# A four-layer graph network on one core: totals by destination and the first layer joined in one stage

## The reference

```python
h = (x @ W).reshape(N, H, C)                      # H = 4 heads, C = 32
alpha = leaky_relu(s_src[row] + s_dst[col], 0.2)
ex = exp(alpha - m[row])
alpha_n = ex / denom[row]                         # softmax over the edges of one source
msg = alpha_n[:, :, None] * h[col]
out = segment_sum(msg, col, num_segments=N)       # sum over the edges of one destination
x = layernorm(x + out.reshape(N, H * C) + bias)
```

## Time and profile before

| | us |
|---|---|
| median of 3 runs (lowest to highest) | 5147.29 (5142.84 to 5148.02) |
| span of the profiled execution, first to last instruction | 5144.9 |
| stage `gat_sums` in it, 2125.0 to 2191.2 | 66.2 |
| stage `first_layer`, 2191.2 to 2475.7 | 284.5 |
| busy over the span: PE, DVE, ACT, POOL | 3166.0, 3394.4, 2871.6, 3664.3 |

### The profile page before, as it was taken

One profiled execution on the slowest core, in us unless ns is written; L12 is line 12 of the kernel. 1 busy time (PEld: TensorE's weight loads), 2 busy tenths in 40 slices (PEclk: granted clock), 3 DMA queues, 4 the chain that ended last, 5 costly groups with the idle time before them and its releaser, 6 DMA issues. The chain is left out here.

```text
span 5144.9 us, 72170 instructions
## 1 busy us (share of the span) xinstructions
PE 3166.0 (62%) x15758; PEld 2414.5 (47%) x15758; DVE 3394.4 (66%) x11785; ACT 2871.6 (56%) x7156; POOL 3664.3 (71%) x3635
## 2 busy tenths in 40 slices
PE   3555555545652666166476746666988887777774
PEld 3554555523431444155465634544555465555552
DVE  6587566658886777467499973333777776666664
ACT  0114666638874888268367762333555566666663
POOL 5777777767774777378677717776777677777777
PEclk9655555569996888689689978888555599989887
DMA  2336888858872777356478858887677632222222
GB/s 72 78 80 197 250 251 255 251 126 249 251 232 76 226 229 225 96 166 203 133 207 222 222 171 235 225 224 202 197 206 205 180 74 73 72 72 71 71 73 60
DMA packets 820080, 862.65 MB, mean 168 GB/s; under 512 B 161384, under 2 KB 595149, under 8 KB 819227
## 3 DMA queue, kind: packets, MB, share of 16 engines
q1 hardware_dynamic: 703656, 673.59, 42.6%
q0 software_dynamic: 112896, 179.36, 15.5%
q10 hardware_dynamic: 3314, 7.36, 0.4%
HBM read 494.63 MB, written 370.82 MB: 168 GB/s over the span
## 5 line engine op out<-in xcount | busy, mean ns | idle before, releaser
L1929 POOL DMA_INDIRECT gs_xs<-t_t,kept_idx_b x392 | 370.0, 944 | 228.4 <-issue 118.9
L1035 POOL DMA_INDIRECT t_alpha<-gsm_raw,gsm_edge_idx x392 | 386.2, 985 | 165.6 <-issue 117.0
L2193 POOL DMA_INDIRECT mss_xs<-t_x,kept_idx_a x392 | 387.8, 989 | 144.2 <-issue 118.5
L2049 POOL DMA_INDIRECT gs_xs<-t_z,kept_idx_a x392 | 384.5, 981 | 138.3 <-issue 119.2
L2185 POOL DMA_INDIRECT out_dram<-mss_o,kept_scat_idx x392 | 394.9, 1007 | 119.4 <-issue 117.9
L1227 PE MATMUL gsm_hp<-kept_w,gsm_zT 128*128 128x128 f32 x1568 | 252.5, 309 | 357.9 <-ACT gsm_zT L1093 357.5
L1025 POOL DMA_INDIRECT gsm_raw<-t_al,kept_idx_b x392 | 379.0, 967 | 124.5 <-issue 118.5
L1598 POOL DMA_INDIRECT att_xs<-t_t,kept_idx_a x392 | 371.5, 948 | 134.2 <-issue 117.3
L536 POOL DMA_INDIRECT sort_xs<-in_x_dram,kept_src_idx x392 | 379.8, 969 | 119.5 <-issue 119.5
L534 POOL DMA_INDIRECT sort_xd<-in_x_dram,kept_dst_idx x392 | 378.7, 966 | 119.4 <-issue 119.4
L216 PE MATMUL gs_tp<-kept_ident,gs_xs 128*128 128x128 f32 x784 | 277.5, 370 | 263.6 <-DMA gs_xs<-t_t,kept_idx_b 154.6
(11 more groups left out here) (556 smaller groups left out, 11014.5 us busy)
## 6 DMA issues: line engine op xcount, KB each, us to landing
t_t<-sort_o SPq DMA_DIRECT2D x61, 858.0 KB
t_x<-gsm_o SPq DMA_DIRECT2D x196, 264.0 KB
sort_x<-in_x_dram SPq DMA_DIRECT2D x61, 832.0 KB
gsm_x<-t_t SPq DMA_DIRECT2D x196, 256.0 KB
t_z<-gsm_z SPq DMA_DIRECT2D x196, 256.0 KB
out_dram<-gsm_o SPq DMA_DIRECT2D x196, 256.0 KB, 3.1
t_t<-l_o SPq DMA_DIRECT2D x49, 528.0 KB, 3.1
att_own<-t_t SPq DMA_DIRECT2D x98, 264.0 KB
```

What stands on the lines that cost most here:

```text
L1035: pool.indirect_dma_start(T["alpha"], bass.IndirectOffsetOnAxis(edge_idx[:, c:c + 1], 0), raw[:, c, :], None).then_inc(scattered[u], 16)
L1929: pool.indirect_dma_start(xs[u][:, j, :], None, T["t12"], bass.IndirectOffsetOnAxis(K["idx_b"][:, c:c + 1], 0)).then_inc(gathered[u], 16)
L2049: pool.indirect_dma_start(xs[u][:, j, :], None, T["z1"], bass.IndirectOffsetOnAxis(K["idx_a"][:, c:c + 1], 0)).then_inc(gathered[u], 16)
L2193: pool.indirect_dma_start(xs[q % BUFS][:, j, :], None, T["x3"], bass.IndirectOffsetOnAxis(K["idx_a"][:, c:c + 1], 0)).then_inc(gathered[q ...
```

## The change

`gat_sums` and `first_layer` become one stage, `totals_and_first_layer`.

- The totals are kept as rows of 512 edges (98 rows used), so a row is four blocks of 128 that TensorE turns from SBUF. The six stores and six loads through DRAM are gone. The degree is scanned first, from ones; the four heads follow, read straight from the loaded table. GpSimd clears 32 partitions of that table.
- TensorE turns the items 0 to 4 between the turns of the scans and item 5 behind the heads, ScalarE copies them, GpSimd shifts them. There are ten `x` buffers, seven of transposed `x`, three of `o`, three double ones of `y`.
- The 15 instructions of the index tables stand in seven groups in the loop, every fourth slot; the five root tables stand behind the loop.
- The norm's statistics lie in SBUF (PSUM is now full), are made for two items at a time, and need no copy.
- A third of the shifts (from item 8 on, `q % 3 == 2`) is VectorE's, with a copy of the bias in PSUM.
- The order is written out by `in_slots`, without a loop; product and scale run six slots behind the transposes.
- In `gat_softmax` one turn and four instructions for the table `last` go, and the destination's flags are 512 wide.

The diff, cut to its core:

```diff
-            sp.wait_ge(totals_ready, 1)
-            for h in all_rows:
-                sp.dma_start(T["totals"][h].rearrange("(p f) -> p f", f=CHUNKS), v[:, h, :]).then_inc(totals_stored, 16)
-            sp.wait_ge(totals_stored, 16 * (HEADS + 2))
-            for h in all_rows:
-                sp.dma_start(rows[0:quarter, h, :], T["totals"][h].rearrange("(r f) -> r f", f=4 * P)).then_inc(rows_loaded, 16)
...
+AHEAD = 6
+X_TILES = 10
+TURNED_TILES = AHEAD + 1
+TABLES_FROM = AHEAD + 8
+def shift_by_vector(q):
+    return q >= AHEAD and q % 3 == 2
...
+        side = ps("side", [P, 4, P])
+        bias = side[:, 1, :]
...
+            load(0)
+            sp.wait_ge(raw_zero, 1)
...
+            parts = [(load, 0, 1, EIGHTS), (store, LOAD_LEAD + AHEAD + 5, 1, EIGHTS)]
...
+        def _(pool):
+            def shift(q):
+                if not shift_by_vector(q):
+                    pool.wait_ge(turned, q + 1)
+                    pool.tensor_tensor(x[q % X_TILES][:], x[q % X_TILES][:], K["bias0"][:].unsqueeze(1).broadcast_to([P, G, D]), ALU.add).then_inc(shifted_by_pool, 1)
...
+            pool.memset(raw[96:P], 0.0).then_inc(raw_zero, 1)
+            pool.wait_ge(raw_zero, 1)
+            in_slots((add, AHEAD + 1, 1, EIGHTS), (shift, 0, 1, EIGHTS))
...
+            segment_scan(dve, link, turner, K["seg"], "sum", counts[:], ones[:])
+            segment_scan(dve, link, turner, K["seg"], "rise", degree[:], counts[:], each=degree_ready)
+            dve.wait_ge(degree_turned, 1)
+            dve.tensor_copy(K["totB"][:, HEADS, :].rearrange("p (r b) -> p b r", b=4), spare[:, :, 0:rows]).then_inc(degree_taken, 1)
+            dve.wait_ge(raw_loaded, 48)
+            segment_scan(dve, link, turner, K["seg"], "sum", run[:], raw[:, :, 0:HEADS].rearrange("p f h -> p h f"))
+            segment_scan(dve, link, turner, K["seg"], "rise", tot[:], run[:], each=head_ready)
...
+            def measure(k):
+                v, wide = k % 2, slice(0, size_of(k))
+                dve.wait_ge(counted, min(2 * k + 2, EIGHTS))
+                even, odd = stats[v][:, wide, 0:3], stats[v][:, wide, 3:6]
+                dve.tensor_tensor(diff[v][:, wide], even[:, :, 1], odd[:, :, 1], ALU.subtract)
+                dve.tensor_tensor(total[v][:, wide], even[:, :, 1], odd[:, :, 1], ALU.add)
+                link(dve.tensor_tensor(var[v][:, wide], even[:, :, 2], odd[:, :, 2], ALU.add))
+                link(dve.scalar_tensor_tensor(out=diff[v][:, wide], in0=diff[v][:, wide], scalar=D / 4.0, in1=diff[v][:, wide], op0=ALU.mult, op1=ALU.mult))
+                dve.tensor_tensor(var[v][:, wide], var[v][:, wide], diff[v][:, wide], ALU.add).then_inc(measured, 1)
...
+            in_slots((count, AHEAD + 2, 1, EIGHTS), (scale, AHEAD, 1, EIGHTS), (measure, AHEAD + 3, 2, PAIRS), (shift, 0, 1, EIGHTS),
+                     (norm_scales, AHEAD + 4, 2, PAIRS), (index_tables, TABLES_FROM, 4, 7), first=AHEAD)
+            dve.wait_ge(square_roots_ready, 1)
+            link(dve.reciprocal(K["dinvB"][:], K["dsqrtB"][:]))
...
+            in_slots((multiply, AHEAD, 1, EIGHTS), (turn, 0, 1, EIGHTS), first=AHEAD)
...
+            in_slots((copy, 0, 1, EIGHTS), (root, AHEAD + 3, 2, PAIRS), (apply, AHEAD + 4, 1, EIGHTS), first=AHEAD)
```

More of the change, by code:

```diff
@@ L855, with segment_tiles @@
 QUARTER = CHUNKS // 4
[L858 to L864, removed]
+def segment_tiles(sb, name, heads, width=CHUNKS, of_maxima=True):
+    seg = {"heads": heads, "width": width, "of_maxima": of_maxima}
+    for tile in ("cont", "nxt", "pre", "suf") + (("negcont", "negpre") if of_maxima else ()):
+        seg[tile] = sb(f"{name}_{tile}", [P, width])
     for row in ("first", "end", "full", "link", "neglink", "a", "nega", "arev", "linkn", "b", "c"):
@@ L962, in segment_scan @@
         else:
-            link(dve.scalar_tensor_tensor(out=o, in0=seg["suf"][:], scalar=carried, in1=o, op0=ALU.mult, op1=ALU.max if kind == "rise" else ALU.add))
+            link(dve.scalar_tensor_tensor(out=o, in0=seg["suf"][:], scalar=carried, in1=o, op0=ALU.mult, op1=ALU.max))
+        if each is not None:
+            dve.sem_inc(each, 1)
 def gat_softmax(nc, A, T, K):
@@ L1435, in norm_apply, with in_slots @@
     ac.then_inc(norm["normed"][u], 1)
-def first_layer(nc, A, T, K):
+def in_slots(*parts, first=0, last=None):
+    for s in range(first, max(lag + every * (count - 1) for _, lag, every, count in parts) + 1 if last is None else last):
+        for f, lag, every, count in parts:
+            if s >= lag and (s - lag) % every == 0 and (s - lag) // every < count:
+                f((s - lag) // every)
+AHEAD = 6
+X_TILES = 10
+TURNED_TILES = AHEAD + 1
+PAIRS = -(-EIGHTS // 2)
+LOAD_LEAD = 2
+TABLES_FROM = AHEAD + 8
@@ L1486, in multiply @@
[L1486 to L1492 removed]
+                    tr = pe.transpose(tp[:, j, :], x[q % X_TILES][:, j, :], K["ident"][:])
+                tr.then_inc(turned, 1)
@@ new lines, in multiply @@
+            def multiply(q):
+                pe.wait_ge(copied, q + 1)
+                if q >= 2:
+                    pe.wait_ge(scaled, q - 1)
+                for j in range(G):
+                    mm = pe.matmul(hp[q % 2][:, j, :], xT[q % TURNED_TILES][:, j, :], K["wh"][:], start=True, stop=True)
+                mm.then_inc(multiplied, 1)
+            turn_by_tensor(pe, turner, K["ident"], last=4)
+            pe.wait_ge(degree_ready, 1)
+            for b in range(4):
+                tr = pe.transpose(spare[:, b, :], degree[:, 0, b * P:(b + 1) * P], K["ident"][:])
@@ new lines, in _ @@
+            tr.then_inc(degree_turned, 1)
+            turn(0)
+            turn(1)
+            turn_by_tensor(pe, turner, K["ident"], first=4, last=6)
+            turn(2)
+            turn(3)
+            turn(4)
+            turn_by_tensor(pe, turner, K["ident"], first=6, last=8)
+            for h in range(HEADS):
+                pe.wait_ge(head_ready, h + 1)
+                for b in range(4):
+                    tr = pe.transpose(hp[h // 2][:, 4 * (h % 2) + b, :], tot[:, h, b * P:(b + 1) * P], K["ident"][:])
+                tr.then_inc(heads_turned, 1)
@@ L1532 @@
 assert BLOCKS * BLOCK == ITEMS
-def in_slots(*parts):
-    for s in range(max(lag + every * (count - 1) for _, lag, every, count in parts) + 1):
-        for f, lag, every, count in parts:
-            if s >= lag and (s - lag) % every == 0 and (s - lag) // every < count:
-                f((s - lag) // every)
 def attention(nc, A, T, K):
```

386 lines of the change are left out of this document (202 added, 184 removed).

## The result

The changed kernel takes 5160.9 us (median of 8 runs, 5157.1 to 5164.9); the kernel before takes 5146.7 on the same chip. The ratio is 1.0027, with a 95% interval of 1.0019 to 1.0035: slower by 14 us. Forecast were 5107 and, as the most likely sign, faster. The profiled execution has a span of 5158.3 us.

The account below looks back on a forecast made before the run. The prediction took a one-engine-at-a-time start and GpSimd's loop as the bound. Start 48.2, loop 240 (VectorE at 4.75 per item) and tail 21 gave 309.2 us instead of 350.7, so 5107 us; range 5066 to 5160.

Parts of the forecast that it names:

- The start: From the new stage's start to its first product by the totals: 48.2 us instead of 77.9.
- The shifts' collision: At the start, VectorE's scans lose time beside GpSimd's five shifts: 5 us taken, between 0 and 11.6.
- That the small instructions and GpSimd shut each other out: In the loop, VectorE instructions with both operands in SBUF meet GpSimd's and wait between 0 and 2.31 us.
- B: Rival, chance 0.27: small loop instructions don't wait, ScalarE sets 4.4 us per item, 5071 us in all.
- By this a VectorE chain with gaps of 0.04 us pays once, at its head: In the loop, a run of closely spaced VectorE instructions waits for GpSimd only at its first instruction.
- In an odd slot the chain of five starts first and pays nothing: In the loop's odd slots, five small VectorE instructions precede GpSimd's add and wait 0, unless a shift still runs.
- The term of 0.8 us of waits per item: In the loop, VectorE's waits for GpSimd, 4.8 us over six slots, added to its 3.95 us of work.
- turning point: Waits in the loop of 1.6 us per item would make the new stage as long as the old.
- VectorE's own work: In the loop, VectorE's instructions without waits take 3.95 us per item.
- Rival D: Chance 0.12: GpSimd gets the port at each semaphore inside VectorE's chain; period 7.4 us, 5237 us in all.
- Rival C: Chance 0.15: GpSimd's add and the following shift let nothing between; 5.6 us per item, 5151 us, no change.
- The tail: From the last product by the totals to the next stage: 21 us, 3 more than before.

Follow-up runs that it names:

- psum_all: The changed kernel with the norm's small tiles in free PSUM and the copy of half the statistics as before; 5072.1 us, ratio 0.9859 to the kernel before.
- old_sbuf: The kernel before with only the first layer's small norm tiles moved from PSUM to SBUF; 5200.6 us, ratio 1.0109 to the kernel before.
- six_more: The changed kernel with six more small VectorE additions ahead of the chain, written to tiles nobody reads; 5189.9 us in one run.
- shifts_late: The changed kernel with GpSimd's first shifts held until the four heads are turned; 5157.0 us, ratio 1.0025 to the kernel before.
- pool_shifts: The changed kernel with the norm's small tiles in PSUM and all 49 shifts on GpSimd; ratio 0.9890 to the kernel before.

## Why the prediction was wrong

- **The start** came out right, 49.3 for 48.2, but by luck: two errors of it cancel. The shifts' collision cost 9.6 us instead of 5. From the end of the last correction (2173.78) to the first product by the totals took 5.0 us instead of 8.2, since item 5's transpose took 1.20 instead of 1.9 and the product 1.95 instead of 3.8, at a granted clock of 1.00; and the heads' scans began 0.7 us sooner than counted.
- **That the small instructions and GpSimd shut each other out** was right (`psum_all`, `old_sbuf`), and B, without waits, fell. `psum_all` takes 5072.1 us where B had 5071, but that agreement is chance: its start is 49.6 for B's 43.2, its stage 284.3 for 274, and its loop holds waits of the index instructions.
- **The step that failed** is "By this a VectorE chain with gaps of 0.04 us pays once, at its head", and with it "In an odd slot the chain of five starts first and pays nothing". It was read from one pair of long instructions beside a gather's issue. In the changed kernel the head pays nothing in most slots, but the add, ready 0.14 us behind the product's end, gets in behind the third small instruction, and the fourth waits (21 times of 25), the fifth too where a shift follows (6 of 25). The term of 0.8 us of waits per item measured 2.3. The offset's part of it was nearly right, 0.9 us per item for the 0.8 that came mostly from it; what failed is the chain's part, put at almost nothing and measured at 1.4. The prediction's turning point was 1.6.
- **VectorE's own work** was put too high, 3.95 us per item, which hid a part of the error. With 2.3 us of waits the prediction's sum would give 48 x 6.25 + 12 = 312 us for a loop that took 293.5. VectorE is busy for 287 of these; less 109 us of waits that fall in the loop and 13 of index instructions and their copy, that leaves 3.4 us per item (an estimate). One reason is in the rows: behind a product the next instruction starts after 1.12 us (2309.51 to 2310.63), where the sum counted 1.26.
- **Rival D** named the place (L1485, L1486 and the offset) and the sign, but its reason, that GpSimd gets the port at each semaphore, is refuted by `old_sbuf` and `six_more`: the instruction that happens to stand next when GpSimd's is ready waits, with a semaphore or without. Its price was too high, 7.4 us per item, since L1486 pays only where a shift is queued behind the add (mean 0.70 instead of 2.3).
- **Rival C**, that an add and the shift behind it let nothing between, happens (6.56 us in `shifts_late`, 7.79 in `pool_shifts`), but the steady chain of the changed kernel gets an instruction through: L1485 ends with the add, and L1486 waits for the shift.
- **The tail** was 2.6 us longer than forecast: 1.6 go with the waits (22.0 in `psum_all`), the other 1.0 stays without them, since ScalarE still has about as many applies to do behind the last product.
- **The root tables** were covered, the index instructions and their copy cost 13 us for 12, and loads and stores did not join, as forecast.

## What to carry to other kernels

Before moving a small tile from PSUM to SBUF, look for GpSimd instructions that read SBUF beside it: each VectorE instruction with both inputs in SBUF may then last as long as a GpSimd one (0.17 us became 2.2), and the wait lands on whichever VectorE instruction is next when GpSimd's becomes ready. If PSUM is full, put the small instructions ahead of the one that releases GpSimd, not behind it (worth half as much here). Don't estimate such waits by laying out slots from one pair of rows: one edit that puts the operands back shows the whole price.

## What the runs showed of the hardware

- The wait is one-sided for short instructions. GpSimd's adds never took over 2.41 us in the changed kernel (median 2.36), so a chain of 0.17 us instructions delays them by 0.05 at most, while VectorE waits a whole add. Long instructions cost both: four scans beside shifts took 9.0 instead of 4.9 us, and three of the five shifts 2.52 to 2.84 instead of 2.36. The Trainium skill says in "SBUF — State Buffer", section "Who interferes with whom", that whoever issues first has the shared ports for its whole instruction. These runs agree for one instruction; that a chain doesn't keep them, and that a waiting VectorE instruction can be passed over by two more GpSimd ones (6.56 us) or three more (7.79), they add.
- One operand in PSUM ends the wait for two-input instructions, as large as scans of 512 columns (2.25 us on average in SBUF beside shifts, 1.21 with the flags in PSUM).
- Copies and casts with one input in SBUF, which write SBUF, wait too: four columns took 2.0 us (L933 above) instead of 0.17, and the cast L1506 4.4 and 7.8 us instead of 0.36. With the small tiles in PSUM such waits of the index instructions are what is left in the loop, 23 of their 30.1 us (an estimate, less the 7.2 that they took before); no run moves these instructions.
